# Cross-attention's causal mask: from TensorE products into the VectorE instruction that takes the row maxima

## Chip, cores and metric

One core of one Trainium2 chip (trn2) runs the whole program. The metric is the device time of that core in microseconds (us), taken as the median over several runs; lower is better.

## What is computed

One decoder layer over 16 sequences of 128 tokens with 256 channels, in three stages, each with a layer norm ahead of it and a residual behind it. The first is a retention (scores times a decay table, per-head normalisation, a gate), the second a causal cross-attention, the third an FFN with one expert for every two sequences. The change lies in the second:

```python
qh = (q @ Wq + bq).reshape(b, s, H, HD).transpose(0, 2, 1, 3)   # H = 16 heads of HD = 16
kh = (k @ Wk + bk).reshape(b, s, H, HD).transpose(0, 2, 1, 3)
scores = jnp.einsum('bhqd,bhkd->bhqk', qh, kh) * HD ** (-0.5)
causal = jnp.triu(jnp.ones((s, s), dtype=bool), k=1)
scores = jnp.where(causal, -jnp.inf, scores)
attn = jax.nn.softmax(scores, axis=-1)
out = jnp.einsum('bhqk,bhkd->bhqd', attn, vh)
```

## The kernel before

**Tiling and stages.** The 16 sequences are taken two at a time, in 8 steps. The stages are a software pipeline: round `i` runs stage A (retention) of step `i`, stage B (cross-attention) of step `i - 1` and stage C (FFN) of step `i - 2`. `pipeline` calls `body` for rounds 0, 1 and 2, loops over rounds 3 to 6, and calls it for rounds 7, 8 and 9. So stage B runs in rounds 1 to 8. Round 1 has no stage C, round 8 no stage A; rounds 2 to 6 hold all three and the preparation of the next stage A, round 7 all three without that preparation.

**Order.** There is no scheduler. Each engine (TensorE = PE, VectorE = DVE, ScalarE = ACT, GpSimd = POOL, SyncE = SP for DMAs) has its own instruction stream, written out by hand in its `body`, and runs it strictly in that order. Semaphores tie the streams together: `s_S` (scores written), `s_max` (maxima taken), `s_prob` (exponentials written), `s_T` (exponentials transposed), and so on.

**Scores.** A step has 2 sequences with 16 heads each, that is 32 score tiles of 128 x 128. They are handled in 8 units `u` of `G = 4` heads; a unit fills one PSUM bank (128 x 512 fp32). Units 0 to 3 belong to the first sequence, 4 to 7 to the second. The query weights carry a minus sign and the scale, so the banks hold negated scores, and the row maximum is a minimum. `scores(bk)` on PE (line 1158) first writes the mask to its four banks, one product each of a bf16 identity with the mask `mask_bf` (0 on and below the diagonal, 1e30 above, repeated for four heads), and then adds 16 products of queries and keys to them.

**Softmax of a unit.** `maxima(u)` on DVE (line 824) takes the four minima of the bank's rows with one `tensor_reduce` over 128 x 512. `exps(u)` on ACT (line 550) makes four ACTIVATE instructions of 128 x 128, one for each head, since the bias is that head's minimum: `exp(-s + min)`, from the bank in PSUM to the SBUF buffer `prob` (four units deep). `prob_transposes(u)` on PE (line 1187) transposes the four heads to bank `b1k`; ACT (even units) or DVE (odd units, `probT_odd`) copies them to `probT`; `with_values(u)` (line 1199) multiplies with the values, to which a column of ones is joined for the denominators.

**DVE's order around it**, in a full round (lines 971 to 1023): maxima 0 and 1; `split_hidden(c, 2)` (two instructions, `h_hi` and `h_lo`, lines 818 and 821); maxima 2 and 3; `split_hidden(c, 3)`; `probT_odd(1)`; the variances and the statistics of the next `x` (lines 986, 759 to 766); maxima 4; `probT_odd(3)`; maxima 5; `rnA` (line 1005); maxima 6 and 7; the normalisation of the next `x` (line 774); `outT` (line 1019); `probT_odd(5)`.

**PE's order around it** (lines 1401 to 1475): `scores(0)`; the retention's products; `down(0)`, `down(1)` (the FFN's second product in pieces); transposes 0; a transpose for stage A; `down(2)`; transposes 1; `down(3)`, which needs `h_lo` of `split_hidden(c, 3)`; transposes 2; values 0 and 1; `down(4)`; `scores(1)`; transposes 3; `down(5)`; transposes 4; values 2 and 3; transposes of `rnA`; transposes 5; `down(6)`; `values_to_tokens(0)`; then the product of `outT` with `W2_sb`, which needs DVE's `outT`; transposes 6; and on.

Of the kernel before, what the change touches and what calls it, by code (L numbers as in the profile page):

```python
# [25 lines left out]
BF16 = mybir.dt.bfloat16  # L26
# [3 lines left out]
P = 128  # L30
# [9 lines left out]
G = 4  # L40
# [22 lines left out]
def decoder_kernel(nc, x, ctx_in, Wq, Wk, Wv, W1, W2, gn_w, gn_b, xWq, xbq, xWk, xbk, xWv, xbv, xWo, xbo,  # L63
                   w1, b1, w2, b2, decay, out):
    ctx = ExitStack()
    with ctx:
# [11 lines left out]
        ident_bf = sb("ident_bf", [P, P], BF16)  # L78
        mask_bf = sb("mask_bf", [P, G, P], BF16)
        decay_sb = sb("decay_sb", [P, RH, P])  # L80
# [318 lines left out]
        def _(pool):  # L399

            pool.memset(ident[:, :], 0.0).then_inc(s_const, 1)
            pool.memset(ident_bf[:, :], 0.0).then_inc(s_const, 1)
            pool.memset(mask_bf[:, :, :], 0.0).then_inc(s_const, 1)
            pool.wait_ge(s_const, 3)
            for m in (ident, ident_bf):
                pool.affine_select(out=m[:, :], in_=m[:, :], compare_op=ALU.not_equal, fill=1.0, base=0,
                                   pattern=[[-1, P]], channel_multiplier=1).then_inc(s_const, 1)
            pool.affine_select(out=mask_bf[:, :, :], in_=mask_bf[:, :, :], compare_op=ALU.is_ge, fill=MASKED,
                               base=0, pattern=[[0, G], [-1, P]], channel_multiplier=1)\
                .then_inc(s_const, 1)  # L410
            pool.memset(minus_half[:, :], -0.5).then_inc(s_const, 1)
# [103 lines left out]
        def _(act):  # L515
# [3 lines left out]
            def body(i, do_a, do_b, do_c, nextA):  # L519
# [30 lines left out]
                def exps(u):  # L550
                    act.wait_ge(s_max, 8 * b + u + 1)
                    if u >= PR or later(b):
                        act.wait_ge(s_T, 8 * b + u - PR + 1)
                    for g in range(G):
                        ins = nc.scalar.activation(prob[:, u % PR, g, :], score_banks[u][:, g * P:(g + 1) * P],  # L555
                                                   ACT.Exp, bias=negmax[:, u, g:g + 1], scale=-1.0)
                    ins.then_inc(s_prob, 1)
# [197 lines left out]
        def _(dve):  # L755
# [26 lines left out]
            def body(i, do_a, do_b, do_c, nextA):  # L782
# [41 lines left out]
                def maxima(u):  # L824
                    dve.wait_ge(s_S, 2 * b + u // PR + 1)
                    if u == 0 and later(b):
                        dve.wait_ge(s_prob, 8 * b)
                    nc.vector.tensor_reduce(negmax[:, u, :], score_banks[u][:, :].rearrange("p (g m) -> p g m", g=G),  # L828
                                            AX_X, ALU.min).then_inc(s_max, 1)

# [272 lines left out]
        def _(pe):  # L1103
# [35 lines left out]
            def body(i, do_a, do_b, do_c, nextA):  # L1139
# [18 lines left out]
                def scores(bk):  # L1158

                    banks = (S_BANK if do_a else S_LAST)[PR * bk:PR * (bk + 1)]  # L1160
                    if bk == 0:
                        pe.wait_ge(s_qcopy, b + 1)
                        pe.wait_ge(s_kcopy, b + 1)
                        if do_a:
                            pe.wait_ge(s_scD, RJ * (a + 1))
                        else:
                            pe.wait_ge(s_att, 2 * b)
                            pe.wait_ge(s_pvT, 2 * b)
                            pe.wait_ge(s_x1, b + 1)
                    elif do_a:  # L1170
                        pe.wait_ge(s_prob, 8 * b + PR)
                    else:
                        pe.wait_ge(s_attTlo, b)
                        pe.wait_ge(s_x2, b)
                        pe.wait_ge(s_prob, 8 * b + 2)
                    for bank in banks:
                        mm(bank[:, :], ident_bf[:, :], mask_bf[:, :, :].rearrange("p g m -> p (g m)"),
                           start=True, stop=False)
                    tok = slice(bk * P, (bk + 1) * P)
                    for cc in range(C):  # L1180
                        for r in range(PR):
                            rows = slice(XG * r, XG * (r + 1))
                            ins = mm(banks[r][:, cc * 2 * P:(cc + 1) * 2 * P].rearrange("p (h m) -> p h m", h=2),
                                     qB[rows, cc, tok], kB[rows, :, cc, tok], start=False, stop=(cc == C - 1))
                    ins.then_inc(s_S, 1)
# [128 lines left out]
                if not do_a:  # L1314
# [8 lines left out]
                    prob_transposes(3)  # L1323
                    pe.wait_ge(s_prob, 8 * b + 3)
                    ffn_input(b3)
# [3 lines left out]
                    pe.wait_ge(s_xTClo, c + 1)  # L1329
                    pe.wait_ge(s_prob, 8 * b + 4)  # L1330
                    up(0, UP_BEFORE_LAST[0])
                    values_to_tokens(0)
                    prob_transposes(5)
                    with_values(4)
                    pe.wait_ge(s_prob, 8 * b + 5)
# [4 lines left out]
                    pe.wait_ge(s_prob, 8 * b + 6)  # L1340
                    up(2, UP_BEFORE_LAST[2])
                    with_values(6)
                    with_values(7)
                    pe.wait_ge(s_prob, 8 * b + 7)
# [3 lines left out]
                    pe.wait_ge(s_prob, 8 * b + 8)  # L1348
                    attention_transposes(c0)
# [126 lines left out]
                if do_b and not nextA:  # L1476
                    pe.wait_ge(s_prob, 8 * b + 7)
                    context(b0)
# [87 lines left out]
```

## Time and profile before

| | us |
|---|---|
| median of 3 runs | 389.2 (385.6 to 390.26) |
| the profiled execution, its own time | 386.52 |
| its span in the profile | 384.3 |
| between two successive full rounds | 42.47 |
| PE busy in such a round | 40.84 |
| DVE busy in such a round | 30.26 |
| ACT busy in such a round | 29.67 |

A round is taken from one maxima of unit 4 to the next (188.27 to 230.74 us from the span's start). The granted clock of TensorE in these rounds is 1.00 of full speed. The chain of work that ended last gives PE 78% of the span, DVE 7% and ACT 7%.

### The profile page before, as it was taken

Reading aid. Unit: us, or ns where it says so; the run is one execution under the profiler, and the core shown is the slowest. Engines: PE = TensorE matmul, PEld = TensorE weight load, DVE = VectorE, ACT = ScalarE, POOL = GpSimd, SP = SyncE. Lnnn points to the kernel's source line nnn. Section 1 sums busy time; section 2 is a strip of 40 time slices with the busy share of each in tenths; the row PEclk is TensorE's granted clock in tenths of the full one; section 3 lists DMA queues with packets and bytes.
Section 4 is the critical chain, followed back from the end, with each engine's and each line's share of the span. In section 5 each row is a group of like instructions: output and inputs, shape, how many; then the busy total and the mean of one; then the engine's idle time right before and its main releaser. Section 6 shows DMA issues by size and latency. Waiting matters only on the chain.

```text
span 384.3 us, 8935 instructions
## 1 busy us (share of the span) xinstructions
PE 338.0 (88%) x3258; PEld 283.3 (74%) x3273; DVE 257.0 (67%) x564; ACT 237.1 (62%) x578; POOL 163.4 (43%) x145
## 2 busy tenths in 40 slices
PE   0846867999999998999999998999899998879787
PEld 0745745798779876898679877898689877757687
DVE  3575648567766685668756777669756766483775
ACT  1223247577685687577676768578666765687641
POOL 3113306435561636435572636254563551146350
PEclk9977989999999999999999999999999999999999
DMA  7633100212204040044004030134004300003300
GB/s 219 175 87 123 27 2 3 97 41 57 82 3 162 20 138 0 29 151 136 0 10 167 5 132 0 53 124 136 0 14 166 109 2 15 29 1 125 109 29 27
DMA packets 22313, 26.95 MB, mean 70 GB/s; under 512 B 2896, under 2 KB 20112, under 8 KB 22288
## 3 DMA queue, kind: packets, MB, share of 16 engines
q1 hardware_dynamic: 20384, 26.51, 21.4%
q10 hardware_dynamic: 1904, 0.10, 0.3%
q8 instruction: 16, 0.26, 0.3%
q14 instruction: 9, 0.07, 0.1%
HBM read 24.51 MB, written 2.10 MB: 69 GB/s over the span
## 4 chain that ended last, share of the span: by engine, by line
PE 78%; DVE 7%; ACT 7%; issue 4%; DMA 2%; POOL 1%; ACTq 0%; DVEq 0%
PE c L1105 22%; PE a L1105 16%; PE b L1105 13%; PE b1k L1196 7%; PE b1k L1105 6%; PE b2k L1105 5%; ACT prob L555 3%; DMA wv_c<-in_L_attn_Wv 2%; ACT probT L517 2%; DVE negmax L828 2%; PE c L1223 2%; PE a L1120 1%; DVE scD L809 1%; PE b2k L1120 1%; PE a L1424 1%
## 5 line engine op out<-in xcount | busy, mean ns | idle before, releaser
L555 ACT ACTIVATE prob<-b,negmax 128x128 f32<-128x128 f32 x124 | 36.0, 392 | 33.5 <-DVE negmax L828 33.5
L426 POOL TENSOR_TENSOR w_lo<-w_in,w_hi 128x512 fp32r<-128x512 f32 x32 | 40.9, 1309 | 33.9 <-ACT w_hi L517 30.7
L1196 PE MATMUL b1k<-ident,prob 128*128 128x128 f32 x256 | 40.3, 280 | 14.3 <-ACT probT L517 6.4
L432 POOL TENSOR_TENSOR w_lo<-w_in,w_hi 128x512 fp32r<-128x512 f32 x28 | 35.5, 1287 | 28.7 <-ACT w_hi L517 26.9
L419 POOL TENSOR_TENSOR rstA<-varA,minus_half 128x16 f32<-128x16 f32 x8 | 23.4, 2927 | 52.9 <-DVE varA L988 52.9
L1196 PEld LDWEIGHTS b1k<-ident,prob 128*128 128x128 f32 x256 | 28.0, 140 | 24.2 <-ACT prob L555 10.4
L517 ACT ACTIVATE w_hi<-w_in 128x512 fp32r<-128x512 f32 x64 | 38.8, 643 | 2.6 <-PE b L1105 2.6
L828 DVE TENSOR_REDUCE negmax<-b 128x4 f32<-128x512 f32 x31 | 21.3, 686 | 20.7 <-PE b2k L1105 14.9
L1105 PE MATMUL c<-xTC_hi,w_hi 128*128 128x256 f32 x108 | 31.8, 294 | 0.8 <-DVE xTC_lo L779 0.7
L1105 PE MATMUL c<-w_hi,h_hi 128*128 128x256 f32 x96 | 30.9, 322 | 0.0
L1105 PE MATMUL c<-xTC_lo,w_hi 128*128 128x256 f32 x108 | 30.5, 282 | 0.0
L1105 PE MATMUL c<-xTC_hi,w_lo 128*128 128x256 f32 x108 | 30.4, 282 | 0.0
L835 DVE COPY probT<-b1k 128x512 f32<-128x512 f32 x32 | 22.0, 687 | 11.7 <-PE b1k L1196 11.5
L532 ACT ACTIVATE h_in<-c,b_cur 128x256 f32<-128x256 f32 x54 | 22.7, 473 | 11.3 <-PE c L1105 11.1
L1105 PE MATMUL c<-w_hi,h_lo 128*128 128x256 f32 x96 | 26.9, 280 | 0.0
L1105 PE MATMUL c<-w_lo,h_hi 128*128 128x256 f32 x96 | 26.9, 280 | 0.0
L821 DVE TENSOR_TENSOR h_lo<-h_in,h_hi 128x512 fp32r<-128x512 f32 x32 | 24.5, 766 | 1.1
L419 POOL TENSOR_TENSOR rsC<-mvC,minus_half 128x2 f32<-128x2 f32 x8 | 5.7, 712 | 45.7 <-DVE mvC L766 45.7
L1105 PEld LDWEIGHTS c<-xTC_hi,w_hi 128*128 128x128 f32 x108 | 20.5, 190 | 2.7 <-issue 1.5
L517 ACT ACTIVATE probT<-b1k 128x512 f32<-128x512 f32 x32 | 20.5, 639 | 2.5 <-PE b1k L1196 2.5
L1105 PEld LDWEIGHTS c<-w_hi,h_hi 128*128 128x128 f32 x96 | 18.0, 188 | 3.8 <-issue 2.4
L1105 PEld LDWEIGHTS c<-xTC_lo,w_hi 128*128 128x128 f32 x108 | 20.6, 191 | 0.0
(286 smaller groups left out, 1115.1 us busy)
## 6 DMA issues: line engine op xcount, KB each, us to landing
w_in<-in_L_ffn_w SPq DMA_DIRECT2D x16, 1024.0 KB, 5.4
x_in<-in_x SPq DMA_DIRECT2D x8, 256.0 KB, 2.8
c_in<-in_ctx SPq DMA_DIRECT2D x8, 256.0 KB, 2.9
out<-x2b SPq DMA_DIRECT2D x7, 256.0 KB, 2.2
b_cur<-in_L_ffn_b SPq DMA_DIRECT2D x8, 128.0 KB, 3.1
W_sb<-in_L_attn_W SPq DMA_DIRECT2D x2, 256.0 KB, 5.0
decay_sb<-in_decay SPq DMA_DIRECT2D x1, 512.0 KB, 6.1
w_in<-in_L_xattn_Wq SPq DMA_DIRECT2D x1, 256.0 KB, 6.6
```

What stands on the lines that cost most here:

```text
L419: pool.tensor_tensor(out, in_, minus_half[:, 0:n], ALU.pow).then_inc(s_out, 1)
L426: pool.tensor_tensor(w1_lo[:, :, part], w1_in[:, :, part], w1_hi[:, :, part].bitcast(F32), ALU.subtract).then_inc(s_w1lo, 1)
L432: pool.tensor_tensor(w2_lo[:, part, :], w2_in[:, part, :], w2_hi[:, part, :].bitcast(F32), ALU.subtract).then_inc(s_w2lo, 1)
L517: nc.scalar.activation(out, in_, ACT.Copy).then_inc(done, 1)
L532: ins = nc.scalar.activation(h_in[:, u, k, :], bank[:, k * T:(k + 1) * T], ACT.Gelu_apprx_tanh, bias=b1_cur[:, f:f + 1])
L555: ins = nc.scalar.activation(prob[:, u % PR, g, :], score_banks[u][:, g * P:(g + 1) * P], ACT.Exp, bias=negmax[:, u, g:g + 1], scale=-1.0)
L821: nc.vector.tensor_tensor(h_lo[:, part, :], h_in[:, u, :, :], h_hi[:, part, :].bitcast(F32), ALU.subtract).then_inc(s_hlo, 1)
L828: nc.vector.tensor_reduce(negmax[:, u, :], score_banks[u][:, :].rearrange("p (g m) -> p g m", g=G), AX_X, ALU.min).then_inc(s_max, 1)
L835: nc.vector.tensor_copy(probT[:, u % PR, :, :], b1k[:, :].rearrange("p (g n) -> p g n", g=G)).then_inc(s_pTd, 1)
L1105: return nc.tensor.matmul(out, lhsT, rhs, start=start, stop=stop)
L1120: ins = nc.tensor.transpose(out[:, col:col + P], src[:, b, k * P:(k + 1) * P], ident[:, :])
L1196: ins = nc.tensor.transpose(b1k[:, g * P:(g + 1) * P], prob[:, u % PR, g, :], ident[:, :])
```

## The change

The mask product of each bank is dropped, and the score products start their bank themselves. The mask is now one fp32 tile of 128 x 128, `mask_f`, in SBUF. `maxima(u)` is four instructions, one for each head: each reads 128 x 128 scores from PSUM and the mask from SBUF, adds them, writes the sum to `prob` in SBUF, and puts the running minimum (started at 1e30) in one column of `negmax`. The exponentials read `prob` and write it in place. The wait for the buffer to be free (`s_T`) moves from ACT to DVE. As the banks are read last by DVE now, the waits of PE for a free bank go from `s_prob` to `s_max` (also in the rounds 7 and 8, six more places that are not all shown).

```diff
-        mask_bf = sb("mask_bf", [P, G, P], BF16)
+        mask_f = sb("mask_f", [P, P])
...
                 def exps(u):
                     act.wait_ge(s_max, 8 * b + u + 1)
-                    if u >= PR or later(b):
-                        act.wait_ge(s_T, 8 * b + u - PR + 1)
                     for g in range(G):
-                        ins = nc.scalar.activation(prob[:, u % PR, g, :], score_banks[u][:, g * P:(g + 1) * P],
+                        ins = nc.scalar.activation(prob[:, u % PR, g, :], prob[:, u % PR, g, :],
                                                    ACT.Exp, bias=negmax[:, u, g:g + 1], scale=-1.0)
                     ins.then_inc(s_prob, 1)
...
                     if u == 0 and later(b):
                         dve.wait_ge(s_prob, 8 * b)
-                    nc.vector.tensor_reduce(negmax[:, u, :], score_banks[u][:, :].rearrange("p (g m) -> p g m", g=G),
-                                            AX_X, ALU.min).then_inc(s_max, 1)
+                    if u >= PR or later(b):
+                        dve.wait_ge(s_T, 8 * b + u - PR + 1)
+                    wait_apart(dve)
+                    for g in range(G):
+                        ins = nc.vector.tensor_tensor_reduce(
+                            out=prob[:, u % PR, g, :], in0=score_banks[u][:, g * P:(g + 1) * P], in1=mask_f[:, :],
+                            scale=1.0, scalar=MASKED, op0=ALU.add, op1=ALU.min, accum_out=negmax[:, u, g:g + 1])
+                    ins.then_inc(s_max, 1)
...
                     elif do_a:
-                        pe.wait_ge(s_prob, 8 * b + PR)
+                        pe.wait_ge(s_max, 8 * b + PR)
                     else:
                         pe.wait_ge(s_attTlo, b)
                         pe.wait_ge(s_x2, b)
-                        pe.wait_ge(s_prob, 8 * b + 2)
-                    for bank in banks:
-                        mm(bank[:, :], ident_bf[:, :], mask_bf[:, :, :].rearrange("p g m -> p (g m)"),
-                           start=True, stop=False)
+                        pe.wait_ge(s_max, 8 * b + 2)
                     tok = slice(bk * P, (bk + 1) * P)
                     for cc in range(C):
                         for r in range(PR):
                             rows = slice(XG * r, XG * (r + 1))
                             ins = mm(banks[r][:, cc * 2 * P:(cc + 1) * 2 * P].rearrange("p (h m) -> p h m", h=2),
-                                     qB[rows, cc, tok], kB[rows, :, cc, tok], start=False, stop=(cc == C - 1))
+                                     qB[rows, cc, tok], kB[rows, :, cc, tok], start=True, stop=True)
                     ins.then_inc(s_S, 1)
```

## Rows read from the trace of the kernel before

**Rows 1.** The page, part 1: busy time, share of the span, instructions.

```profile
PE 338.0 (88%) x3258; PEld 283.3 (74%) x3273; DVE 257.0 (67%) x564; ACT 237.1 (62%) x578; POOL 163.4 (43%) x145
```

**Rows 2.** Busy us (instructions) of a full round: PE, PEld, DVE, ACT, POOL; clock, DMA.

```profile
188.27:230.74 42.47, 40.84 (x407) 34.57 (x409) 30.26 (x67) 29.67 (x72) 20.82 (x18) 1.00 0.22 71
```

**Rows 3.** The chain of work, this round: start us, us, engine, tile, line.

```profile
188.27 0.70 DVE negmax L828
189.26 0.89 ACT prob L555 x3
190.19 0.66 PE b1k L1196 x4
...
192.63 0.66 PE b1k L1196 x4
...
219.02 0.38 PE b2k L1105
219.40 0.22 PE b L1105
219.61 0.22 PE a L1105
219.83 0.41 PE b L1105
...
225.65 0.96 PE c L1105 x6
...
230.74 0.70 DVE negmax L828
```

**Rows 4.** PE's timeline: the `outT` product, a mask product, the first score product.

```profile
194.27 1.89 PE L1105 MATMUL a<-W_sb,outT 128*128 128x256 f32 x8
...
219.02 0.38 PE L1105 MATMUL b2k<-mask_bf,ident_bf 128*128 128x512 bf16 x1
...
219.76 0.48 PE L1105 MATMUL b<-kB,qB 32*128 32x256 f32 x1
```

**Rows 5.** DVE's timeline: two stretches of this round.

```profile
192.51 0.87 DVE L1019 SCALAR_TENSOR_TENSOR outT<-a,gn_sb,silA 128x256 f32<-128x256 f32 x2
...
206.26 0.75 DVE L759 BATCH_NORM_STATS2 statC<-x 128x6 f32<-128x256 f32 x2
207.17 0.25 DVE L763 BATCH_NORM_AGGREGATE mvC<-statC 128x2 f32<-128x6 f32 x2 [0.16 <-DVE statC L759]
...
220.97 0.69 DVE L828 TENSOR_REDUCE negmax<-b 128x4 f32<-128x512 f32 x1 [0.33 <-PE a L1105]
...
223.24 0.68 DVE L828 TENSOR_REDUCE negmax<-b 128x4 f32<-128x512 f32 x1
223.84 0.68 DVE L828 TENSOR_REDUCE negmax<-a 128x4 f32<-128x512 f32 x1
224.44 0.42 DVE L818 TENSOR_SCALAR h_hi<-h_in 128x512 fp32r<-128x512 f32 x1
224.89 0.69 DVE L821 TENSOR_TENSOR h_lo<-h_in,h_hi 128x512 fp32r<-128x512 f32 x1
```

**Rows 6.** Groups of DVE by line and shape: busy us, mean ns, idle before.

```profile
L759 DVE BATCH_NORM_STATS2 statC<-x 128x6 f32<-128x256 f32 x16 | 6.0, 417 | 0.2
...
L763 DVE BATCH_NORM_AGGREGATE mvC<-statC 128x2 f32<-128x6 f32 x16 | 2.0, 165 | 1.3 <-DVE statC L759 1.3
...
L1092 DVE TENSOR_REDUCE head_of<-ident 128x2 f32<-128x128 f32 x1 | 0.3, 280 | 0.0
```

**Rows 7.** Groups of ACT by line and shape, the same columns.

```profile
L517 ACT ACTIVATE w_hi<-w_in 128x512 fp32r<-128x512 f32 x64 | 38.8, 643 | 2.6 <-PE b L1105 2.6
L555 ACT ACTIVATE prob<-b,negmax 128x128 f32<-128x128 f32 x124 | 36.0, 392 | 33.5 <-DVE negmax L828 33.5
...
L517 ACT ACTIVATE xTA<-a 128x512 f32<-128x512 f32 x8 | 4.8, 598 | 11.1 <-PE a L1120 11.1
```

**Rows 8.** DVE's timeline in round 8: first maxima, and the split that releases PE.

```profile
336.45 0.69 DVE L828 TENSOR_REDUCE negmax<-b 128x4 f32<-128x512 f32 x1 [0.70 <-PE a L1105]
...
346.23 0.69 DVE L779 TENSOR_TENSOR xTC_lo<-b,xTC_hi 128x512 fp32r<-128x512 f32 x1 [0.38 <-ACT xTC_hi L517]
```

More of the change, by code:

```diff
@@ L402, in _ @@
             pool.memset(ident_bf[:, :], 0.0).then_inc(s_const, 1)
-            pool.memset(mask_bf[:, :, :], 0.0).then_inc(s_const, 1)
+            pool.memset(mask_f[:, :], 0.0).then_inc(s_const, 1)
             pool.wait_ge(s_const, 3)
@@ L407, in _ @@
                                    pattern=[[-1, P]], channel_multiplier=1).then_inc(s_const, 1)
-            pool.affine_select(out=mask_bf[:, :, :], in_=mask_bf[:, :, :], compare_op=ALU.is_ge, fill=MASKED,
-                               base=0, pattern=[[0, G], [-1, P]], channel_multiplier=1)\
-                .then_inc(s_const, 1)
+            pool.affine_select(out=mask_f[:, :], in_=mask_f[:, :], compare_op=ALU.is_ge, fill=MASKED,
+                               base=0, pattern=[[-1, P]], channel_multiplier=1).then_inc(s_const, 1)
             pool.memset(minus_half[:, :], -0.5).then_inc(s_const, 1)
@@ L1323, in body @@
                     prob_transposes(3)
-                    pe.wait_ge(s_prob, 8 * b + 3)
+                    pe.wait_ge(s_max, 8 * b + 3)
                     ffn_input(b3)
@@ L1329, in body @@
                     pe.wait_ge(s_xTClo, c + 1)
-                    pe.wait_ge(s_prob, 8 * b + 4)
+                    pe.wait_ge(s_max, 8 * b + 4)
                     up(0, UP_BEFORE_LAST[0])
@@ L1334, in body @@
                     with_values(4)
-                    pe.wait_ge(s_prob, 8 * b + 5)
+                    pe.wait_ge(s_max, 8 * b + 5)
                     up(1, UP_BEFORE_LAST[1])
@@ L1339, in body @@
                     prob_transposes(7)
-                    pe.wait_ge(s_prob, 8 * b + 6)
+                    pe.wait_ge(s_max, 8 * b + 6)
                     up(2, UP_BEFORE_LAST[2])
@@ L1343, in body @@
                     with_values(7)
-                    pe.wait_ge(s_prob, 8 * b + 7)
+                    pe.wait_ge(s_max, 8 * b + 7)
                     up(3, UP_BEFORE_LAST[3], (0,))
@@ L1347, in body @@
                     up(3, UP_BEFORE_LAST[3], (1,))
-                    pe.wait_ge(s_prob, 8 * b + 8)
+                    pe.wait_ge(s_max, 8 * b + 8)
                     attention_transposes(c0)
@@ L1476, in body @@
                 if do_b and not nextA:
-                    pe.wait_ge(s_prob, 8 * b + 7)
+                    pe.wait_ge(s_max, 8 * b + 7)
                     context(b0)
```

## The prediction

> **What bounds the kernel now.** I read the page's busy shares first: PE is busy for 338.0 of 384.3 us, DVE for 257.0, ACT for 237.1 [rows 1]. Then the busy time by stretch: in a full round of 42.47 us PE works 40.84, DVE 30.26, ACT 29.67, at the full clock [rows 2]. So PE idles for only 1.6 us in a round, and DVE for 12.2. Third the chain of work. It runs through PE nearly everywhere, and at one place leaves it: behind `scores(1)` PE has to wait for maxima 4 on DVE (188.27), the exponentials on ACT, and takes up the transposes at 190.19 and again, after a copy, at 192.63 [rows 3]. Last the timeline of DVE, for what stands behind the maxima in its order; there two deadlines of PE show. The first is `down(3)` at 225.65 [rows 3]: the `h_lo` that it needs ends at 224.89 + 0.69 = 225.58 [rows 5]. There is no slack at all. The second is the product of `outT`: PE starts it at 194.27 [rows 4], `outT` is ready at 192.51 + 0.87 = 193.38 [rows 5], 0.9 us earlier. So DVE, two thirds busy, is already level with PE in the stretch that the change makes longer.
>
> **What goes.** 8 mask products in a round, 64 in all. In the chain they stand as pieces of 0.38, 0.22 and 0.22 ahead of the scores [rows 3] (a fourth has no row). What a group of four costs is the time from the first mask product to the first score product, 219.76 - 219.02 = 0.74 us [rows 4]; the start that the mask makes now, the scores make then. Two groups: 1.48 us a round, at most 8 x 1.48 = 11.8 us in all. That is the whole gain. The waits that change from `s_prob` to `s_max` give nothing in rounds 2 to 7, as PE works right up to `scores(1)`; in round 8 `scores(1)` is released earlier, but DVE becomes the bound there (below). The smaller mask set-up on POOL lies under the first loads.
>
> **What comes: the size of a unit on DVE.** Let U be the time by which one `maxima` moves on what stands behind it on DVE. Now one reduction of 128 x 512 does so by 223.84 - 223.24 = 0.60 us [rows 5] (it takes 0.69, the tail overlaps with the next). The new instruction, with a second operand from SBUF, a stored result and a running minimum, is nowhere in this trace, so I bound it. Two statistics of 256 columns take 0.75 together, one alone 0.417, so one moves the next by 0.33 [rows 5, 6]. From 256 to 512 columns that is 0.27 us, 1.04 ns a column; so 128 columns move it by 0.20, of which some 0.07 do not depend on size. Four of them: U = 0.80, the lower end, if storing the minimum is free. If storing it is a small operation of its own, the nearest row is the aggregate: two take 0.25, one 0.165, so 0.085 each [rows 5, 6], and U = 4 x (0.20 + 0.085) = 1.14. If nothing overlaps, 4 x (0.280 + 0.165) = 1.78, with the 280 ns of the one 128 x 128 reduction [rows 6]; that is the upper end. I take 1.14: a single running value has to leave the engine after the last element, and the row of a few columns is what such a thing looks like.
>
> The Trainium skill (VectorE: DVE Perf Modes, section on two Vector instructions with no wait between them) says that an operation which also writes its accumulator is two instructions, the main one and an accumulator read. It gives no time for the read; by that rule U = 0.80 is out, and no row of this trace shows it. The same page's rules for kernel authors say to minimise the count of DVE operations; here one becomes four (or eight), which by that rule costs, where the port of the mask to DVE looks free by busy shares.
>
> **What comes: ACT.** The exponentials read SBUF instead of PSUM. Copies of 512 columns take 643 ns from SBUF and 598 from PSUM [rows 7], 45 ns more, so 0 to 1.4 us on 32 exponentials a round. ACT idles 12.8 us a round; on the chain to the transposes it adds at most 0.2 us for a unit of four. I count it as nothing, since by the sums below it is DVE that PE waits for, and that path has no exponential in it; with U = 0.80 that cover is thin and it would cost some 0.2 us a round.
>
> **Sum for a full round.** Three terms.
> 1. `scores(0)` is done 0.74 earlier.
> 2. From maxima 0 to maxima 4. Now 230.74 - 220.97 = 9.77 us [rows 3, 5]. DVE goes from maxima 0 to the end of `h_lo` in 225.58 - 220.97 = 4.61, of which four maxima are 2.40: so 2.21 + 4U. Then PE goes from `down(3)` to the next maxima 4 in 230.74 - 225.65 = 5.09, less 0.74 for the second group of masks: 4.35. With 0.05 between them the new stretch is 6.6 + 4U, a change of 4U - 3.17. Queued behind `down(3)` on PE are transposes 2, values, `down(4)` and `scores(1)`, so all of them are late.
> 3. From maxima 4 to the `outT` product. Now 194.27 - 188.27 = 6.00. DVE: 193.38 - 188.27 = 5.11 with four maxima in it, so 2.71 + 4U, and 0.1 to PE's start: a change of 4U - 3.2 once U is over 0.85. Below that the path over exponentials and transposes ends last, at 0.2 over today for U = 0.80.
>
> Together 8U - 7.1 for a round. With U = 1.14 that is **+2.0 us**; it is zero at U = 0.89; with 0.80 it is -0.5, with 1.78 +7.1. After the `outT` product PE is busy without a gap until the next `scores(0)`, so nothing is given back.
>
> **The other rounds** at U = 1.14. Rounds 2 to 6 have the sum: 5 x 2.0 = 10.0. Round 7 has no normalisation ahead of `outT`, about 0.6 less: +1.4. Round 1 has no hidden halves to be late; it gains 1.5, pays one longer unit ahead of the exponentials (0.5) and about 1.2 behind `scores(1)`: some +0.3 (an estimate). Round 8: seven units lie between the first maxima and the split that frees PE, 346.23 - 336.45 = 9.78 [rows 8]; with 1.6 us of gaps in it that is 4.0 + 7U of work, 12.0, starting 0.74 earlier: +1.5. Sum: 13.2 us on the profiled execution's 386.5, 399.7 us. The median of the runs lies 2.7 above that execution, so I name 401.
>
> **The rivals.**
> - *The minimum is stored for free* (U near 0.80). For it: the reduction now stores four values without showing any cost. Against it: there the values are the output itself. Rounds 2 to 7 give -0.5 each, rounds 1 and 8 about -0.9 each: -4.8, 382 to 384 us, within 2%.
> - *Nothing overlaps* (U from 1.46, where the store starts only at the end of the main part, to 1.78). For it: dependent operations here do wait, as the gap of 0.16 between statistics and aggregate shows [rows 5]. Against it: that gap is a wait on a semaphore, and here none is written between the four. Four to eight steps of U give 5 x 7.1 + 6.4 + 3.5 + 6.1 = +51 at 1.78 (438 us), and +32 at 1.46 (419 us).
> - *Faster: PE gets its products back and DVE hides the rest.* It ends on the other side. Needed is that DVE never comes late, which is U up to about 0.65, by less fixed cost in each instruction than the 256-column rows show. For it: DVE idles 12.2 us a round [rows 2]. Against it: four times 128 columns cannot be quicker than 512 unless the 0.07 of fixed cost goes. Full gain: 386.5 - 11.8 = 374.7 us, -3.1%.
> - *The mask products hid something*: if the first score product had to wait anyway (for weights, or the bank), the 0.74 does not come back. The time would be up to 11.8 above the forecast, 411 us. Against it: the products stand back to back in the chain ahead of the scores [rows 3]. I count it within the slow side.
>
> **How the numbers follow.** Forecast, U from 1.0 to 1.3, 392 to 411 us: 0.50. Store for free, U from 0.8 to 1.0, 380 to 392 us: 0.22. No overlap or masks not returned, above 411 us: 0.20. The faster rival: 0.08. About 2% is what a measurement of this kernel can tell from no change; of 389.2 that is 381.4 to 397.0. Faster: the 0.08 and a fifth of the second case, 0.12. Same: the rest of the second and the quarter of the first under 397, 0.30. Slower: 0.58. The range of 382 to 425 leaves out the faster rival and the far end of the slow one, some 0.2. Of the likeliest case alone the range is 392 to 411.
>
> **What would show it.** In the changed kernel's trace: no mask rows, and the first score product some 0.35 us behind the last `up` product; DVE with four instructions of about 0.28 to 0.30 us for a unit, and either small operations between them or not: their start-to-start time times four is U, and the round should be 42.47 + 8U - 7.1. DVE's busy time in a round should rise from 30.3 to some 35 to 38. PE should stand idle ahead of `down(3)` on `h_lo` (1.6 us at U = 1.14) and ahead of the `outT` product. Wrong would be the forecast if the round falls under 42.0, if PE waits for exponentials and not for `h_lo` and `outT`, or if a unit moves DVE by less than 0.9 or more than 1.3 us.

## The result and the profile after

The changed kernel takes 390.67 us (median of 20 runs, 387.9 to 392.92), the kernel before 387.95 (20 runs beside it). The ratio is 1.0063, with a 95% interval of 1.004 to 1.0085: a small loss, under the 2% that count as slower. The forecast was 401, so a loss of 3%; 390.67 lies in its range, but the named size is wrong by more than a factor of four. The profiled execution has a span of 389.0 us (384.3 before). Ratios in this document are of fast runs alone: one run each of e1, e11 and e12 below (379.6, 390.29 and 550.76 us, the last at a mean clock of 0.563) is slow, and is not in them.

The profile page of the changed kernel, busy shares and DVE's two groups of the masked softmax (columns as in [rows 1] and [rows 6]):

```profile
PE 331.6 (85%) x3209; PEld 282.6 (73%) x3209; DVE 270.9 (70%) x1012; ACT 245.1 (63%) x578; POOL 162.9 (42%) x145
...
L829 DVE CUSTOM_DVE_ANT_0 prob<-b,mask_f 128x128 f32<-128x128 f32 x124 | 28.4, 284 | 15.0 <-PE b2k L1108 13.5
...
L829 DVE DVE_READ_ACCUMULATOR2_ANT negmax<- 128x1 f32 x256 | 20.8, 81 | 0.0
```

DVE has two instructions for each head, 284 and 81 ns, so eight for a unit. What matters is when they start. DVE's timeline of the changed kernel, the first two heads of a unit and the places that answer to [rows 5]:

```profile
223.13 0.76 DVE L818 TENSOR_TENSOR h_lo<-h_in,h_hi 128x512 fp32r<-128x512 f32 x1
223.82 0.28 DVE L829 CUSTOM_DVE_ANT_0 prob<-b,mask_f 128x128 f32<-128x128 f32 x1
224.03 0.08 DVE L829 DVE_READ_ACCUMULATOR2_ANT negmax<- 128x1 f32 x1
224.03 0.28 DVE L829 CUSTOM_DVE_ANT_0 prob<-b,mask_f 128x128 f32<-128x128 f32 x1
...
228.71 0.69 DVE L818 TENSOR_TENSOR h_lo<-h_in,h_hi 128x512 fp32r<-128x512 f32 x1
...
233.74 0.29 DVE L829 CUSTOM_DVE_ANT_0 prob<-b,mask_f 128x128 f32<-128x128 f32 x1 [1.64 <-PE b2k L1108]
...
238.97 0.87 DVE L1022 SCALAR_TENSOR_TENSOR outT<-a,gn_sb,silA 128x256 f32<-128x256 f32 x2
```

The masked instructions start 0.21 us apart. The read of the accumulator starts together with the next head's instruction and adds nothing to that distance. So a unit moves what is behind it by U = 4 x 0.21 = 0.84 us, against 0.60 before.

A stretch of one round's length in the busy time, columns as in [rows 2], and PE's timeline with the waits in brackets; behind them PE's timeline of the kernel before at the same place as the second line, and ACT's timelines, before and after:

```profile
197.69:240.28 42.59, 39.43 (x401) 33.95 (x401) 31.93 (x123) 30.68 (x74) 20.84 (x19) 1.00 0.21 71
```

```profile
229.46 0.39 PE L1108 MATMUL c<-w_hi,h_hi 128*128 128x256 f32 x1 [0.56 <-DVE h_lo L818]
...
236.04 0.66 PE L1196 MATMUL b1k<-ident,prob 128*128 128x128 f32 x4 [1.32 <-ACT prob L552]
```

```profile
232.66 0.66 PE L1196 MATMUL b1k<-ident,prob 128*128 128x128 f32 x4 [0.69 <-ACT prob L555]
```

```profile
189.00 1.14 ACT L555 ACTIVATE prob<-b,negmax 128x128 f32<-128x128 f32 x4 [3.49 <-DVE negmax L828]
```

```profile
234.71 1.28 ACT L552 ACTIVATE prob<-prob,negmax 128x128 f32<-128x128 f32 x4 [3.12 <-DVE negmax L829]
```

A round is 42.59 us long where it was 42.47. PE works 1.41 us less in it and idles 1.5 more: 0.56 at `down(3)` on `h_lo`, where it did not wait before; 1.32 at transposes 4 on the exponentials, where it waited 0.69; and 0.20 and 0.28 at transposes 0 and 1. The mask products went, and nearly the same time of waiting came in their place. In the changed kernel's chain DVE has 17% of the span (7% before) and PE 65% (78%).

Where the 4.7 us between the two spans lie, from the starts of the score and `outT` products in PE's timelines: up to the first score (or mask) product of round 1 +1.4, from there to round 1's `outT` product +1.85 (17.03 to 18.88), round 2 -0.3, the next five rounds +0.65 together, the end from round 7's `outT` product on +1.05 (62.86 to 63.91). The first part holds no edit but the set-up of the mask, and ends between 47.1 and 51.1 us in the profiles of this study (49.7 and 49.0 in the two of the kernel before), whatever was changed. What the parts in rounds 1 and 8 are is read in the section on the clock.

### The profile page after: what moved, and what is told of

Its sections match the earlier page's. It is cut to its first block, busy times and chain, and to the rows that moved or that the text cites. A ratio compares the mean times of both kernels' runs of the same rounds, so it can differ in the third digit from the quotient of the medians.

```text
span 389.0 us, 9294 instructions
## 1 busy us (share of the span) xinstructions
PE 331.6 (85%) x3209; PEld 282.6 (73%) x3209; DVE 270.9 (70%) x1012; ACT 245.1 (63%) x578; POOL 162.9 (42%) x145
## 4 chain that ended last, share of the span: by engine, by line
PE 65%; DVE 17%; ACT 8%; issue 7%; DMA 2%; POOL 1%; DVEq 0%; ACTq 0%
PE c L1108 16%; PE a L1108 14%; PE b L1108 12%; DVE prob L829 7%; PE b1k L1108 6%; PE b1k L1196 6%; ACT prob L552 5%; PE b2k L1108 3%; PE c L1223 2%; DMA wv_c<-in_L_attn_Wv 2%; DVE scD L806 2%; PE a L1123 1%; ACT probT L516 1%; DVE h_lo L818 1%; DVE probT L838 1%
## 5 line engine op out<-in xcount | busy, mean ns | idle before, releaser
L552 ACT ACTIVATE prob<-prob,negmax 128x128 f32<-128x128 f32 x256 | 81.2, 392 | 30.5 <-DVE negmax L829 30.5
L1196 PE MATMUL b1k<-ident,prob 128*128 128x128 f32 x256 | 42.8, 292 | 23.8 <-ACT prob L552 13.0
L425 POOL TENSOR_TENSOR w_lo<-w_in,w_hi 128x512 fp32r<-128x512 f32 x32 | 41.1, 1306 | 35.9 <-ACT w_hi L516 31.9
L1196 PEld LDWEIGHTS b1k<-ident,prob 128*128 128x128 f32 x256 | 29.5, 147 | 35.2 <-ACT prob L552 22.4
L829 DVE CUSTOM_DVE_ANT_0 prob<-b,mask_f 128x128 f32<-128x128 f32 x124 | 28.4, 284 | 15.0 <-PE b2k L1108 13.5
L1108 PE MATMUL b<-kB,qB 32*128 32x256 f32 x124 | 19.2, 417 | 2.7 <-DVE scD L806 2.7
L829 DVE DVE_READ_ACCUMULATOR2_ANT negmax<- 128x1 f32 x256 | 20.8, 81 | 0.0
```

The lines of the kernel that those rows point to most:

```text
L425: pool.tensor_tensor(w1_lo[:, :, part], w1_in[:, :, part], w1_hi[:, :, part].bitcast(F32), ALU.subtract).then_inc(s_w1lo, 1)
L552: ins = nc.scalar.activation(prob[:, u % PR, g, :], prob[:, u % PR, g, :], ACT.Exp, bias=negmax[:, u, g:g + 1], scale=-1.0)
L829: ins = nc.vector.tensor_tensor_reduce(out=prob[:, u % PR, g, :], in0=score_banks[u][:, g * P:(g + 1) * P], in1=mask_f[:, :], scale=1.0, s ...
L1108: return nc.tensor.matmul(out, lhsT, rhs, start=start, stop=stop)
L1196: ins = nc.tensor.transpose(b1k[:, g * P:(g + 1) * P], prob[:, u % PR, g, :], ident[:, :])
```

## The experiments

Edits are to the changed kernel unless it says before. The first four ran beside one another, then the next four, then the last four, each group with the kernel before on the same chip. This table, worked out from the timelines of PE and DVE (one full round each, us), is what the readings rest on. The columns: the round; from the `outT` product to the first score product (mask products, where there are any, stand ahead of it); from there to maxima 0; from maxima 0 to maxima 4; from maxima 4 to the next `outT` product. The last two are the second and third term of the prediction's sum.

| kernel | round | to scores 0 | to maxima 0 | maxima 0 to 4 | maxima 4 to `outT` product | median, us |
|---|---|---|---|---|---|---|
| before | 42.46 | 25.49 | 1.21 | 9.77 | 5.99 | 387.95 |
| changed | 42.59 | 24.62 | 1.68 | 9.92 | 6.37 | 390.67 |
| e1, no mask | 41.14 | 24.61 | 1.68 | 8.85 | 6.00 | 375.87 |
| e2, both masks | 44.14 | 25.50 | 1.46 | 10.81 | 6.37 | 400.98 |
| e3, fifth part | 45.13 | 24.71 | 1.68 | 10.76 | 7.98 | 405.47 |
| e4, PSUM in place | 44.42 | 24.72 | 1.69 | 10.34 | 7.67 | 400.90 |
| e5, wait order | 42.50 | 24.61 | 1.69 | 9.83 | 6.37 | 390.66 |
| e6, split first | 42.49 | 24.60 | 1.69 | 9.82 | 6.38 | 390.33 |
| e7, fifth part, norm first | 44.18 | 24.73 | 1.69 | 10.76 | 7.00 | 402.23 |
| e8, three moves | 42.41 | 24.62 | 1.68 | 9.74 | 6.37 | 388.92 |
| e10, six moves | 41.98 | 25.07 | 1.69 | 9.35 | 5.87 | 385.91 |
| e11, copy first | 42.03 | 24.60 | 1.69 | 9.36 | 6.38 | 385.68 |
| e12, before with new order | 41.93 | 25.71 | 1.21 | 9.76 | 5.25 | 384.58 |

### The two halves of the change

**e1: the mask products alone taken out of the kernel before** (the causal mask is left out of the computation).

```diff
-                    for bank in banks:
-                        mm(bank[:, :], ident_bf[:, :], mask_bf[:, :, :].rearrange("p g m -> p (g m)"),
-                           start=True, stop=False)
...
-                                     qB[rows, cc, tok], kB[rows, :, cc, tok], start=False, stop=(cc == C - 1))
+                                     qB[rows, cc, tok], kB[rows, :, cc, tok], start=True, stop=True)
```

> The kernel before without its 64 mask products and with nothing in their place: the causal mask is left out of the computation, everything else, the single reduction per unit too, is as before. It measures the whole gain of dropping the products alone. Theory 1 (the products' time comes back on TensorE as the prediction says, and the longer unit on VectorE and ScalarE eats it): a full round goes from 42.47 to about 41.0 us (two groups of 0.74), all rounds together 10 to 12 us, some 376 us. Theory 2 (the products hid something, a wait for weights or banks, and the changed kernel is level simply because neither half of the change moved anything): a round stays above 42.0 us and the time within 4 us of the kernel before.

Measured: ratio 0.9663 (0.9605 to 0.972), 375.87 us beside 388.35, so -12.5 us. In the trace a full round is 1.33 us shorter (41.13 or 41.14), PE busy for 39.48 us of it; eight times that is 10.6. The two profiled executions, at mean clocks of 0.963 and 0.982, are only 8.3 apart in span, and runs at the same clock of 0.973 some 12 us. Theory 2 and the prediction's last rival (the products hide something) fall: their time comes back nearly whole. Not quite, at `scores(0)`: they start 0.88 earlier, but maxima 0 only 0.41, since DVE is still at the `h_lo` of the second hidden part (the first rows of the changed kernel's timeline above show the same: `h_lo` from 223.13, maxima 0 at 223.82, the scores done at 223.3). That limit the prediction had not seen. The second group gives back more than the 0.74 that it was put at: from `down(3)` to maxima 4 takes 4.21 us in e1 and 5.09 before, so 0.88.

**e2: the changed kernel with the mask products put back.**

```diff
+                    for bank in banks:
+                        mm(bank[:, :], ident_bf[:, :], mask_bf[:, :, :].rearrange("p g m -> p (g m)"),
+                           start=True, stop=False)
...
+                                     qB[rows, cc, tok], kB[rows, :, cc, tok], start=False, stop=(cc == C - 1))
```

> The changed kernel with the mask products on TensorE put back, so that the mask is added twice (the result stays the same): the VectorE half of the change alone, as a cost. Theory 1: a full round of the changed kernel is 42.59 us, and the two groups of products add 1.3 to 1.5, so about 44.0 us, and some 402 us in all, +13 to 14 on the kernel before. Theory 2 (neither half moves much): a round under 43.0 us, under 395 us.

Measured: ratio 1.0342 (1.0282 to 1.0402), 400.98 us, +12.6. PE's list of work is that of the kernel before, with 41.17 us busy in a full round (40.84 before), and the round is 1.68 longer. So the level result is the difference of two large terms: -12.5 for the products, +12.6 for the masked minimum and its exponentials. Taking the products from e2 gives -10.3, and eight rounds by e1's trace -10.6, so the first is rather 10 to 12. As terms of a round (e2 less before): +0.25 from the scores to maxima 0, +1.04 from maxima 0 to 4, +0.38 behind it.

### Was the sum right and only U wrong?

**e3: a fifth instruction in each unit**, its result read by nobody, so that U = 5 x 0.21 = 1.05.

```diff
+                    nc.vector.tensor_tensor_reduce(
+                        out=dump[:, u % 8, :], in0=score_banks[u][:, 0:P], in1=mask_f[:, :],
+                        scale=1.0, scalar=MASKED, op0=ALU.add, op1=ALU.min, accum_out=dump_min[:, u:u + 1])
                     for g in range(G):
```

> The changed kernel with a fifth 128x128 instruction in each unit of maxima, which repeats the first head into a buffer that nobody reads: it sets the size of the unit on VectorE to 1.05 us (measured in the changed kernel: four starts 0.21 apart, 0.84), near the 1.14 that the prediction took. It tells whether the prediction's sum was right and only that size wrong. The sum's slope is 4 in the stretch between the two score blocks and up to 4 behind the second: +0.84 us and +0.4 to +0.84, so a full round of 43.8 to 44.2 us and 400 to 403 us in all. If instead VectorE is off the path in the changed kernel (rival: ScalarE's longer exponentials set it), a round rises by less than 0.4 us, under 394 us.

Measured: ratio 1.0449 (1.039 to 1.0509), 405.47 us, and a round of 45.12 or 45.13, about 1 us beyond what was expected.

From maxima 0 to 4 it took 10.76, +0.84 on the changed kernel, exactly the slope of 4 that the second term has. The excess is behind maxima 4. DVE's timeline there, and GpSimd's beside it:

```profile
292.33 1.71 DVE L773 TENSOR_SCALAR xnA<-x_in,mvA,rsA 128x256 f32<-128x256 f32 x2
```

```profile
292.58 5.17 POOL L427 TENSOR_TENSOR w_lo<-w_in,w_hi 128x512 fp32r<-128x512 f32 x4 [3.69 <-ACT w_hi L518]
```

The two instructions of the normalisation take 1.71 us where they take 0.73 in the changed kernel. They began at 292.33, GpSimd's first `w_lo` at 292.58; of the two the first took 0.41 us, and the second, which began behind GpSimd's start, 1.38. Round 7, which has no normalisation, is 43.74 us long in this kernel.

**e7: the same, with the normalisation ahead of maxima 6 and 7.**

```diff
-                if do_b:
-                    maxima(6)
-                    maxima(7)
                 if nextA and do_b:
                     normalise(a + 1, x_in, mvA, rsA, xnA, s_rsA, s_xnA, s_TA)
+                if do_b:
+                    maxima(6)
+                    maxima(7)
```

> The kernel with the fifth part in each unit (45.13 us a round, 405.5 in all), with the normalisation of the next x on VectorE moved ahead of maxima 6 and 7. In that kernel the two instructions of the normalisation took 1.71 us together, where they take 0.73 in the kernel before and in the changed one, and they lay beside the first of GpSimd's w_lo subtractions. Theory 1 (the two engines shut each other out there, and the longer unit pushed VectorE into GpSimd's stretch): ahead of maxima 6 GpSimd is idle, the pair takes 0.73 again, a round is 1.0 us shorter, 44.1 to 44.2 us, some 399 us in all. Rival (the 1.71 has another cause, such as the fifth part itself): the pair stays near 1.7 us and the round at 45.1.

Measured: 402.23 us, ratio 1.0361 (1.0298 to 1.0424), a round of 44.18. DVE's timeline:

```profile
239.10 0.73 DVE L773 TENSOR_SCALAR xnA<-x_in,mvA,rsA 128x256 f32<-128x256 f32 x2
```

GpSimd's subtractions begin only at 241.45 here, and its instruction ahead of them ends at 237.76. With GpSimd idle beside it the pair takes 0.73 again and the round is 0.95 shorter. Theory 1 holds. The Trainium skill (SBUF — State Buffer, section on SBUF's two separate sides) says that VectorE in a mode that uses both its ports and GpSimd hold a shared pair of ports in turn, each for a whole instruction. The 1.38 us of the second instruction agrees with it: it ended 0.17 us behind the first of GpSimd's four subtractions, which take 1.29 each.

What is left in e7 is the sum's own forecast: 8 x 1.05 - 7.1 = +1.3, measured 44.18 - 42.47 = +1.7. Term by term the second and third hold (+0.99 and +1.01, where the formulas give +1.03 and +1.0), and the first gives 0.3 instead of 0.74. So the sum of a round is sound for a U of this size. In all the kernel takes 402 us; the same working gives some 397 for U = 1.05 (an estimate from the terms of the prediction: 5 x 1.3, +0.7, +0.8 and about nothing in round 1, on 389.2). That 402 is near the 401 named for U = 1.14 is chance.

### Other suspects

**e4: the masked scores written back to PSUM, exponentials from there** (and the banks released by `s_prob` as before).

```diff
-                            out=prob[:, u % PR, g, :], in0=score_banks[u][:, g * P:(g + 1) * P], in1=mask_f[:, :],
+                            out=score_banks[u][:, g * P:(g + 1) * P], in0=score_banks[u][:, g * P:(g + 1) * P], in1=mask_f[:, :],
...
-                        ins = nc.scalar.activation(prob[:, u % PR, g, :], prob[:, u % PR, g, :],
+                        ins = nc.scalar.activation(prob[:, u % PR, g, :], score_banks[u][:, g * P:(g + 1) * P],
```

> The changed kernel, but the masked scores are written back in place to their PSUM bank, and the exponentials read them from there as in the kernel before (so the banks are released by the exponentials again). It tells what the exponentials' source in SBUF costs: four of them take 1.28 us in the changed kernel and 1.14 before. Theory 1: behind the second score block the path runs over two units of exponentials and a copy, so a round gets 0.2 to 0.3 us shorter, about 42.3 us, and 388 to 389 us in all, if VectorE writes PSUM as fast as SBUF. If a write to PSUM is slower there, the unit of 0.84 us grows and the round with it, by 8 times the growth. Rival (the source does not matter, only VectorE does): 42.6 us a round, 390.7 in all.

Measured: ratio 1.0328 (1.0274 to 1.0381), 400.90 us. DVE's groups:

```profile
L829 DVE DVE_READ_ACCUMULATOR2_ANT negmax<- 128x1 f32 x256 | 35.2, 138 | 0.0
L829 DVE CUSTOM_DVE_ANT_0 b<-b,mask_f 128x128 f32<-128x128 f32 x124 | 32.1, 319 | 14.4 <-PE b2k L1108 12.9
```

With PSUM as the target the heads start 0.25 apart, not 0.21, and U is 1.0. That adds 0.42 from maxima 0 to 4, and pushes the normalisation beside GpSimd as in e3 (1.76 us for the pair). Four exponentials take 1.14 to 1.20 us here, so the 1.28 of the changed kernel is the source in SBUF; what that costs in the time this kernel did not tell, since the gain is under the two losses.

**e5: the wait for the scores behind the two waits that are met long before.**

```diff
-                    dve.wait_ge(s_S, 2 * b + u // PR + 1)
                     if u == 0 and later(b):
                         dve.wait_ge(s_prob, 8 * b)
                     if u >= PR or later(b):
                         dve.wait_ge(s_T, 8 * b + u - PR + 1)
+                    dve.wait_ge(s_S, 2 * b + u // PR + 1)
                     wait_apart(dve)
```

> The changed kernel with the wait for the scores moved behind the two waits that are met long before (s_prob, s_T). In the changed kernel the first masked instruction starts 0.32 us after the last score product (the reduction did 0.07 after it). Theory: a good part of the 0.25 us more is the handling of the waits and of the semaphore instruction that stand between; with the scores' wait later, the gap shrinks to 0.2 or less, and a round by 0.1 to 0.2 us, 1 us in all. Rival: the gap is the start of the new kind of instruction itself; it stays at 0.32, and the time at that of the changed kernel.

Measured: 390.66 us, ratio 1.0064 (1.0031 to 1.0098), not to be told from the changed kernel. In the trace the gap from the last score product to maxima 4 goes from 0.32 to 0.23 and the round from 42.59 to 42.50. So 0.09 of the 0.25 is the order of the waits; the rest stays with the semaphore instruction and the start of the new kind, which were not taken apart.

**e6: `split_hidden(c, 3)` ahead of maxima 3. e8: e5, e6 and the normalisation first together. e11: e8 with `probT_odd(1)` ahead of maxima 3.** The order on DVE in e11:

```diff
                 if do_b:
                     maxima(2)
-                    maxima(3)
                 if do_c:
                     split_hidden(c, 3)
                 if do_b:
                     probT_odd(1)
+                    maxima(3)
```

> The changed kernel with split_hidden(c, 3) on VectorE ahead of maxima 3 instead of behind it. In the changed kernel TensorE waits for that h_lo ahead of down(3). If h_lo(3) is the deadline, as the prediction's second term says, it comes 0.84 us earlier; TensorE is then held by the transposes of unit 1 instead, so that a round gets about 0.5 us shorter, 42.1 us, some 3 us in all. Rival: behind it something else ends at the same time (the exponentials of unit 3, which start later by this, or maxima 4), and a round stays at 42.5 or more.

> The changed kernel with all three moves of order: the scores' wait last, split_hidden(c, 3) ahead of maxima 3, the normalisation ahead of maxima 6 and 7. If the mask products' 12.5 us are real gain and the rest of the cost is VectorE's order, this keeps more of it: a round of 41.9 to 42.2 us and 385 to 387 us in all, a little under the kernel before (387.95). If the order is not what costs, it stays at 390.

> The kernel with the three moves of order, and probT_odd(1) ahead of maxima 3, alone. It tells whether the 0.7 us that TensorE lost again behind down(3) in the two kernels with split_hidden(c, 3) first (3.54 us from down(3) to the second scores against 2.82) is the wait of transposes 2 for this copy: then a round is 41.7 us and the time 383 to 385; if not, 42.4 and 389.

Measured: e6 390.33 us, ratio 1.0046 (1.0014 to 1.0077), round 42.49: the expected 0.5 did not come. e8 388.92, 1.0007 (0.9973 to 1.0041), round 42.41: level, above what was expected. e11 385.68, 0.9942 (0.9908 to 0.9976), round 42.03: between its two expectations. PE's timeline, first of e6, then of e11:

```profile
228.12 0.63 PE L1197 MATMUL b1k<-ident,prob 128*128 128x128 f32 x4 [0.56 <-DVE probT L838]
```

```profile
226.11 0.63 PE L1196 MATMUL b1k<-ident,prob 128*128 128x128 f32 x4 [0.17 <-DVE probT L838]
```

In e6 PE no longer waits for `h_lo` but for the next thing behind it in DVE's order, the copy that transposes 2 need, and for just as long, 0.56 us: DVE's order, not one deadline, is what PE meets. With the copy ahead too the wait is 0.17 and the first stretch 0.4 shorter.

### Does another order save the change?

**e10: the changed kernel with six moves** (e11, and maxima 7 behind `outT`, and the copy of `probT` for unit 4 ahead of `pv_out(0)` on ACT). **e12: the kernel before with the same order** (mask products and single reduction kept; the order of the waits does not arise there). **e9: the kernel before once more.** The two moves that e11 has not:

```diff
                 if do_b:
                     maxima(6)
-                    maxima(7)
                 if do_a:
                     dve.wait_ge(s_rnT, a + 1)
...
                 if do_b:
+                    maxima(7)
                     probT_odd(5)
...
-                    pv_out(0)
                     probT_even(4)
+                    pv_out(0)
```

> The kernel with the three moves of order and three more: on VectorE probT_odd(1) goes ahead of maxima 3 (TensorE waited for that copy once h_lo came early), maxima 7 goes behind outT; on ScalarE the copy of probT for unit 4 goes ahead of pv_out(0), since transposes 5 wait for it. Theory (the masked minimum costs only by what stands behind it in VectorE's and ScalarE's order): the first stretch of a round gets 0.7 us shorter, the second 0.3 to 0.5, so a round of 41.2 to 41.4 us and 380 to 383 us in all, under both kernels. Rival (VectorE or ScalarE as a whole is the bound by now): a round stays above 42.0 us, above 386 in all.

> The kernel before, mask products and single reduction kept, with the same new order on VectorE and ScalarE as the kernel of the six moves. It tells whether that order is a gain by itself or only makes room for the masked minimum. In the kernel before TensorE waits for h_lo(3) with no slack, and for the copies behind the second scores; theory: 0.1 to 0.5 us a round, 384 to 388 us in all, and the change on top of the new order is worth 3 to 6 us, where it cost 2.7 in the old order. Rival: the order gives as much here as there, and the change stays a loss in either.

> The kernel before, profiled once more. Its first profile shows a mean clock of TensorE of 0.982, all other kernels of this study 0.956 to 0.966, and they differ in the set-up ahead of round 1 too, where none of them was changed. Theory 1 (part of the lower clock, that of the set-up, is chance from one execution to the next): the set-up up to the first score products takes 49 to 51 us again in no fixed relation to the kernel, and the round stays 42.5. Theory 2 (the longer unit alone lowers the clock): the clock is 0.98 again.

Measured: e10 385.91 us, ratio 0.9982 (0.9945 to 1.0019), round 41.98. e12 384.58 us, ratio 0.9917 (0.9882 to 0.9952), round 41.93. e9 387.99 us, ratio 1.0011 (0.9975 to 1.0046).

The expectation for e10 was too hopeful, and its rival (above 42.0 us, above 386) just missed: maxima 4 to the `outT` product got 0.5 shorter, but the scores then start 0.45 later after it, so PE is no longer without gaps behind the `outT` product. And the rival given for e12 holds: the new order is worth 0.5 us a round in the kernel before too. What e12 was expected to leave for the change, a gain of 3 to 6 us on top of the new order, did not come. The lowest time found is that of e12, with the mask on PE; the masked minimum is level in the full round in both orders (+0.12 and +0.05 us), and in the whole time behind by 2.7 us in the old order and by 1.3 in the new one, which is at the edge of what ten runs tell.

**The clock.** Mean granted clock of TensorE from 45 to 75 us, in which round 1 lies: 0.94 in the three profiles with masks on PE and one reduction (before, e9, e12), 0.89 in e1 and e2, and 0.77 to 0.83 in all that mask on DVE alone. A mean of 0.83 is a third of the stretch at 1.2 GHz instead of 2.4. The busy time of each engine by stretch shows one such place in round 1 (the eighth number is the clock): from the second score block to maxima 4, first before, then changed.

```profile
59.40:61.36 1.96, 1.96 (x20) 1.06 (x20) 0.52 (x5) 0.04 (x1) 1.96 (x1) 1.00 0.00 0
```

```profile
60.98:63.32 2.34, 2.34 (x22) 1.54 (x19) 0.00 (x0) 0.00 (x0) 2.34 (x3) 0.53 0.00 0
```

The stretch has lost its mask products and is longer all the same: its score products take 2.09 us, in a full round 1.14. Another such place is from transposes 4 to the `outT` product. In a full round it takes 4.1 us in both kernels; in round 1 it takes 3.43 us before, at a clock of 1.00, and 4.36 in the changed kernel, at 0.61, where transposes 5 take 1.08 us instead of 0.63. Worked out so for the whole round 1 (an estimate from PE's timelines): the mask products gave 1.5 back, the longer units, the exponentials and the later starts cost 1.1, and the rest of the +1.85, some 2.2 us, is products at 1.2 GHz on the path.

In round 8 it can be set beside profiles without the lower clock. From the first score (or mask) product of round 8 to the end, of the changed kernel and of e11:

```profile
337.96:389.00 51.04, 40.78 (x365) 35.64 (x364) 34.56 (x119) 30.48 (x75) 21.17 (x17) 0.97 0.17 55
```

```profile
332.94:382.70 49.76, 39.44 (x365) 34.47 (x364) 34.39 (x119) 30.41 (x75) 21.18 (x17) 1.00 0.17 57
```

This stretch takes 49.76 to 49.86 us where its mean clock is 1.00 (before, e9, e11) and 51.00 to 51.14 where the clock falls to the lower level once and its mean is 0.96 or 0.97 (changed, e5, e6, e8, e10, and e12, which has the mask on PE). So a fall costs 1.3 us here in either kind of kernel, and the +1.05 of the end is such a fall. What PE did ahead of it, in the changed kernel and in e11:

```profile
346.48 1.08 PE L1196 MATMUL b1k<-ident,prob 128*128 128x128 f32 x4 [2.45 <-DVE probT L838]
```

```profile
341.46 0.63 PE L1196 MATMUL b1k<-ident,prob 128*128 128x128 f32 x4 [2.38 <-DVE probT L838]
```

With the mask on DVE PE waits here for 2.4 us, before for 0.92. In the changed kernel, e5 and e10 the transposes behind that wait are slower already (1.08, 0.97 and 0.95 us); in e11, behind a wait of the same length, they are not.

The loss goes with the clock. Over all runs the mean clock of the changed kernel is 0.947 to 0.969, of the kernel before 0.965 to 0.982, and among the runs of one kernel those with a lower clock are the longer ones (the changed kernel: 387.9 us at 0.969, 392.7 at 0.948). At the same clock the two take the same time: at 0.965 the changed kernel 389.4 us (mean of 5 runs) and the kernel before 389.9 (10 runs beside the experiments), at 0.968 to 0.969 388.3 (3 runs) and 389.0 (20). The median clock is 0.973 in e1, e9 and e12, with one reduction, and 0.953 to 0.968 in all kernels with the masked minimum. That the longer waits of PE lower the clock is likely by this, but argued: no run sets the clock by itself. As for e9, its profile has the clock of 0.982 again, as its second theory says, but its ten runs have 0.965 to 0.982, so a single profile's clock says little.

## Why the prediction was wrong

**What failed is the size of U.** The prediction took "U = 4 x (0.20 + 0.085) = 1.14" as the likeliest; measured is 4 x 0.21 = 0.84. The 0.20 for the main part was right, from the 256- and 512-column rows, with 0.21 measured. The store of the minimum was put at 0.085, which is the time by which one aggregate moves the next [rows 5, 6]. It is an instruction of its own, of 81 ns, but it starts at the same time as the next main part and moves nothing. So the step that failed is that every small instruction behind a main part moves what follows, as one aggregate does another; the row that was taken for it did not answer to it. That 81 ns is near 0.085 is chance: the one is a duration, the other a distance of starts (an aggregate lasts 165 ns). The rival "the minimum is stored for free", at 0.22, is what happened, in U as in the time of its case (380 to 392 us). By the sum's slope the 0.30 is 8 x 0.30 = 2.4 us a round. Two of the prediction's own signs of being wrong came: a unit moves DVE by less than 0.9 us, and PE waits for exponentials. DVE's busy time in a round is 31.9 us, not 35 to 38.

The prediction had named the Trainium skill's rule (VectorE: DVE Perf Modes, section on two Vector instructions with no wait between them) that an operation which writes its accumulator too is two instructions. The trace agrees, with 284 and 81 ns; that U = 0.80 was out did not follow from it.

**The three terms, at the measured U.** The first, "`scores(0)` is done 0.74 earlier": the scores start 0.87 earlier, but maxima 0 only 0.40, since DVE is busy with `h_lo` until then (e1 shows the same 0.41 with the old reduction); 0.34 too much gain. The second, 4U - 3.17 = +0.2: measured +0.15. That this is so close is partly luck, as three things that were left out cancel: the second group of masks gives back 0.88 and not 0.74, PE comes from the late `down(3)` to `scores(1)` in 2.82 us where e1 takes 3.00, and the first masked instruction starts 0.25 later behind the scores. The third, "0.2 over today" on the path over exponentials and transposes: measured +0.38, with PE waiting there and `outT` ready 0.27 early. From maxima 4 to the first exponential it is 0.97 us instead of 0.73, which is the 0.24 by which a unit has grown; from there to transposes 4 it is 1.33 instead of 1.19, which is ACT's four exponentials, 1.28 us instead of 1.14, and these the prediction had put at nothing. Sum: -0.40 + 0.15 + 0.38 = +0.13 a round, measured 42.59 - 42.47 = +0.12; the formula gives -0.4 for U = 0.84. So the mechanism is confirmed (e3 and e7 set U by hand, and the second term moved by exactly four times it), and its constants were 0.5 too low.

**The other rounds.** Rounds 1 and 8 were put at about -0.9 each for a small U. They came out at +1.85 and +1.05 in the profiled executions. Most of the difference is a term that the prediction does not have: it reckoned with the full clock everywhere, as its rows are from a full round, and in both rounds the changed kernel has more products at 1.2 GHz than the kernel before. Without them round 1 comes to -0.4 (the estimate above), and round 8 to -0.2 (e11: 62.67 us from round 7's `outT` product to the end, 62.86 before).

**The sum of the whole.** 399.7 us for the profiled execution and 2.7 more for the median are 402.4, not the 401 that was named; the difference changes nothing above.

**The rivals.** "The mask products hid something" fell with e1. "PE gets its products back and DVE hides the rest" fell: e1 gives the gain of the products (375.87 us, against the 374.7 named), and e2 shows that DVE hides little of the rest: its units are longer by 8 x 0.24 = 1.9 us in a round, and the round is 1.68 longer. "Nothing overlaps" fell with the timeline. That PE would stand at `down(3)` on `h_lo` was right in kind (0.56 us); that it would stand ahead of the `outT` product was not, with U under the 0.9 or so where the two paths cross.

## What to carry to other kernels

Ask of a new instruction by how much it moves the start of the next one, and look for the rows that show starts; its duration, and the number of instructions it splits into, can both be much larger. When work moves from a full engine to one that is two thirds busy, cost it along that engine's order, stretch by stretch: here the products' 1.33 us a round came back, and as much went into two waits, one for what stands behind the maxima in VectorE's order and one for the exponentials. Compare runs at the same granted clock before a small difference is put down to the work in them. Try the new order on the old kernel as well, or its gain is put down to the change.

## What the hardware showed that was not expected

- The fused add-and-minimum of 128 x 128 with its stored minimum: 284 ns and 81 ns, starts 0.21 us apart; with PSUM as its target 319 and 138 ns, starts 0.25 apart (e4).
- Its first instruction behind a wait starts 0.32 us after the last product, where the reduction did after 0.07; 0.09 of that goes when the waits that are long met come first (e5).
- An fp32 normalisation from SBUF to SBUF beside GpSimd's subtraction: 1.71 us instead of 0.73 for the pair. 0.2 us more in each unit was enough to fall into it, and cost 1 us a round (e3, e7).
- Exponentials of 128 x 128 from SBUF: 1.28 us for four, from PSUM 1.14.
- One fall of TensorE's granted clock from 2.4 to 1.2 GHz in round 8: 51.0 to 51.1 us for the stretch instead of 49.8, with the mask on either engine (changed, e5, e6, e8, e10, e12 against before, e9, e11).
